# Filler products in the three waits between TensorE's first steps

## The reference

```python
x = x + mixer(ctx_1024, layernorm(x), ...)
x = x + ffn(layernorm(x), ...)

# mixer: 4 batches, 256 steps, 256 channels, 16 states a channel
x = einsum("bld,ed->bel", hidden, in_proj_w)          # 128 -> 256 channels
x = silu(causal_conv(x, conv_w, 4 taps) + conv_b)     # u
dt_low, B, C = split(einsum("bdl,ed->bel", x, x_proj_w))
dt = softplus(dt_proj_w @ dt_low + dt_proj_b)
state = state * exp(dt * A) + (dt * u) * B            # scan over the 256 steps
y = (sum over states of state * C + D * u) * silu(z)
# ffn: hidden 1024, activations rounded to 8 bits, weights to -1, 0, 1
h = layer_norm(gelu(silu(bitlinear(x, w1, b1))))
out = bitlinear(h, w2, b2)
```

## Time and profile before

| | us |
|---|---|
| median of 3 runs | 188.28 (187.84 to 191.62) |
| the profiled execution, its own time | 188.09 |
| its span, first to last instruction | 186.2 |
| PE, DVE, ACT, POOL busy in the span | 153.8, 155.1, 159.9, 128.8 |
| mean granted TensorE clock | 0.958 |

### The profile page before, as it was taken

One profiled execution on the slowest core, in us unless ns is written; L12 is line 12 of the kernel. 1 busy time (PEld: TensorE's weight loads), 2 busy tenths in 40 slices (PEclk: granted clock), 3 DMA queues, 4 the chain that ended last, 5 costly groups with the idle time before them and its releaser, 6 DMA issues.

```text
span 186.2 us, 3315 instructions
## 1 busy us (share of the span) xinstructions
PE 153.8 (83%) x1161; PEld 113.3 (61%) x1167; DVE 155.1 (83%) x225; ACT 159.9 (86%) x255; POOL 128.8 (69%) x117
## 2 busy tenths in 40 slices
PE   7868999999989989999778999975998946806762
PEld 4646978778777758667555778644856533305541
DVE  0769607898999999899999998999989399999951
ACT  2288968999999999999999999999999976997331
POOL 4002453799684059997999999789979968776860
PEclk9995799999999999999999999999999999995798
DMA  4919997228752400426260232300000000000011
GB/s 153 346 40 339 391 414 325 7 15 296 298 86 38 188 4 0 182 98 179 2 217 16 105 126 107 116 30 0 0 4 0 0 28 28 4 0 0 30 56 58
DMA packets 20192, 20.12 MB, mean 108 GB/s; under 512 B 13448, under 2 KB 16976, under 8 KB 19536
## 3 DMA queue, kind: packets, MB, share of 16 engines
q1 hardware_dynamic: 19584, 19.15, 31.2%
q10 hardware_dynamic: 592, 0.77, 1.2%
HBM read 17.70 MB, written 2.21 MB: 107 GB/s over the span
## 4 chain that ended last, share of the span: by engine, by line
PE 31%; ACT 29%; DVE 18%; issue 13%; POOL 6%; DMA 2%; DVEq 0%; ACTq 0%; POOLq 0%
ACT dA L681 12%; PE ps L517 8%; PE ps L454 7%; PE ps L555 6%; ACT L778 6%; DVE st L956 3%; DVE stats L1026 3%; POOL st L829 3%; PE ps L483 2%; DVE w_raw L1036 2%; DVE am L1051 2%; DVE w_raw L1040 2%; ACT w_raw L714 2%; ACT w_raw L718 2%; PE ps L465 2%
## 5 line engine op out<-in xcount | busy, mean ns | idle before, releaser
L829 POOL TENSOR_TENSOR st<-st,bc 128x1024 f32<-128x1024 f32 x32 | 76.3, 2400 | 21.3 <-DVE st L956 21.1
L956 DVE TENSOR_TENSOR_SCAN st<-dA,ps 128x1024 f32<-128x1024 f32 x32 | 72.2, 2277 | 10.9 <-PE ps L517 9.1
L681 ACT ACTIVATE dA<-dt,negA 128x255 f32<-128x255 f32 x128 | 52.9, 496 | 0.6 <-POOL negA L810 0.6
L517 PE MATMUL ps<-diagB,dtuT 64*128 64x128 f32 x512 | 44.0, 298 | 3.8 <-DVE st L956 2.7
L517 PEld LDWEIGHTS ps<-diagB,dtuT 64*128 64x128 f32 x512 | 33.6, 191 | 17.9 <-issue 8.7
L778 ACT ACT_TABLE_LOAD x29 | 37.2, 1283 | 0.5
L555 PE MATMUL ps<-id_f,st 128*128 128x128 f32 x256 | 33.9, 277 | 2.6 <-POOL st L829 2.6
L555 PEld LDWEIGHTS ps<-id_f,st 128*128 128x128 f32 x256 | 28.1, 141 | 5.7 <-POOL st L829 3.6
L616 PE MATMUL ps<-id_f,w_raw 128*128 128x128 f32 x64 | 10.4, 314 | 9.2 <-POOL w_raw L891 7.6
L592 PE MATMUL ps<-rows_sb,diag 128*128 128x512 f32 x32 | 15.3, 601 | 0.7 <-ACT w_raw L714 0.4
L616 PEld LDWEIGHTS ps<-id_f,w_raw 128*128 128x128 f32 x64 | 8.3, 161 | 11.2 <-issue 9.4
(11 more groups left out here) (107 smaller groups left out, 226.4 us busy)
## 6 DMA issues: line engine op xcount, KB each, us to landing
bc<-spread SPq DMA_DIRECT2D x16, 512.0 KB, 4.0
diagB<-dblocks SPq DMA_DIRECT2D x3, 1024.0 KB, 4.7
rows_sb<-rows SPq DMA_DIRECT2D x1, 1664.0 KB, 15.6
x_nat<-x SPq DMA_DIRECT2D x2, 512.0 KB, 7.2
w_raw<-w1T SPq DMA_DIRECT2D x1, 1024.0 KB, 9.0
w_raw<-w2T SPq DMA_DIRECT2D x1, 1024.0 KB, 11.6
dblocks<-diagB SPq DMA_DIRECT2D x1, 1024.0 KB, 14.5
out<-res SPq DMA_DIRECT2D x8, 128.0 KB, 1.7
```

Source lines behind the costliest of these rows:

```text
L517: mm = nc.tensor.matmul(o[:, i:i + SG // 2, t, r, :], dtuT[rows, b % 2, h, t, :], diagB[rows, b % 2, t, n, :], start=True, stop=True)
L681: e = nc.scalar.activation(dA[:, k % DA_RING, i * L + 1:(i + 1) * L], dt[:, h, b, 1:L], ACT.Exp, scale=negA[:, h, n:n + 1])
L829: tt(s, s, bc[:, ng].rearrange("p s l -> p (s l)"), ALU.mult).then_inc(prod_done, 1)
L956: nc.vector.tensor_tensor_scan(st[:, k % ST_RING, :], dA[:, k % DA_RING, :], slot(k), 0.0, ALU.mult, ALU.add).then_inc(scanned, 1)
```

## The change

`warm(22)` ahead of `xdbl(0)` becomes `warm(27)`, and two more calls are put in: `warm(5)` between `xdbl(0)` and `dtraw(0)`, and `warm(11)` between `b_cols()` and the first step of `PE_AT[0]`. That makes 21 more products. They wait for nothing but their turn on PE, and no other engine's program differs.

```diff
-WARM_FIRST, WARM_SECOND = 11, 22
+WARM_FIRST, WARM_SECOND, WARM_THIRD, WARM_FOURTH = 11, 27, 5, 11
...
             warm(WARM_SECOND)
             xdbl(0)
+            warm(WARM_THIRD)
             dtraw(0)
             b_cols()
+            warm(WARM_FOURTH)
             for k in range(UNITS + 1):
```

## The result

The changed kernel took 194.24 us (192.94 to 195.69, four runs) against 189.05 of the kernel before in the same comparison: a ratio of 1.030, 95% interval 1.018 to 1.041. I had forecast 187.4 with a range to 188.7. It is slower by 5 us where I saw 0.7 less. Four more runs of the same kernel, made later (after_again), gave 187.81, 190.68, 193.63 and 193.81, so the eight executions have their median at 193.7 and spread over 8 us.

What follows compares the result with a forecast made beforehand. PE was taken as the bound after 14.59, slowed by a clock dip. Of 2.5 us gained there, 0.67 was to survive the read into diagB at no filler cost: 188.09 - 0.67 + 0 = 187.42, say 187.4 us, range 185.5 to 188.7.

Steps and rivals of the forecast that it cites:

- The three waits and their fillers: PE's waits of 0.76, 0.66 and 1.28 us before the clock dip: filling costs 0, PE gains 2.5 us.
- Where it stops: At scale_b:8 the read into diagB lands at about 45.6; about 1.8 of 2.5 us becomes a DMA wait.
- the 0.67: Gain in us left at scale_b:8, 46.27 - 45.60, expected to reach the kernel's end.
- A price to weigh: Earlier bc loads beside the read into diagB might delay its landing; taken as none, 0.5 us as upper bound.
- Rival 3: PE's new wait from 43.8 to 45.6 brings its own clock dip: slower, 189 to 190.5 us; chance 0.08.
- Rival 1: The whole 2.5 us comes through past scale_b:8, 185.6 us; chance 0.15, including a part of it.
- Rival 2: No gain, 188.1 to 188.5 us: landing 0.7 us later, or the clock falls as before; chance 0.20 with another rival.
- The range: Whole kernel: 185.5 to 188.7 us, leaving out the slower case with a new clock dip and little else.

Runs made afterwards that it cites:

- hold_bc: The changed kernel with SyncE holding the four bc loads of batch 1 until the read into diagB has landed; 191.67 us.
- order_only: The changed kernel with GpSimd's product of unit 19 held until VectorE's two diagonal tiles are made, new wait unfilled; 190.75 us.
- wait_in_before: The kernel before, without the 21 products, with TensorE at scale_b:8 also waiting for the second bc load of batch 1; 199.3 us.
- zeros_first: The changed kernel with the zeros for dblocks written ahead of the weight loads and rows_sb loaded behind the read of batch 1; 186.48 us.
- after: The changed kernel itself in its first four runs, one of them profiled, against the kernel before; 194.24 us, ratio 1.030.
- first_two_waits: The changed kernel without the 11 products ahead of turn_half(0), so with warm(27) and warm(5) only; 189.47 us.
- fill_new_wait: The changed kernel with 24 more unread products between sum_states(4) and scale_b:8, in the new wait for the read; 190.98 us.
- last_wait_only: The kernel before with only the 11 products ahead of turn_half(0), none added in the other two waits; 189.29 us.
- fill_and_order: fill_new_wait with GpSimd's product of unit 19 also held until VectorE's two diagonal tiles are made; 189.94 us, ratio 1.002.

## Why the prediction was wrong, point by point

- **The three waits and their fillers: right.** The costs were taken at nothing and are 0.02 us; the gain was 2.5 us and is 2.7 (`xdbl:1` at 23.73, foreseen near 23.9). In the four profiles in which the first full clock came at 8.35 to 9.71, in place of 6.8, the filler cost 0.2 to 0.8 at `xdbl(0)`; I had put 0.1 to 0.3.
- **"Where it stops": right in kind, wrong in size.** PE came to `scale_b:8` at 43.7 (43.8 foreseen), and the wait has its place and cause. But I took the landing as fixed at 45.56, and it was 46.64. With that the 0.67 that I carried to the end is below nothing, -0.46. A landing read from one trace can't carry such a sum: in the ten profiles with this order of DMAs the read landed between 44.7 and 48.0.
- **"A price to weigh": the first step that failed.** I took 0 for the earlier `bc` loads beside the read, 0.5 at most; they cost 0.7 (the read took 5.4). That loads beside the read can cost it this much is shown by hold_bc and by the grouping of thirteen reads; how much it is varies (order_only, 0.2). What misled me was one read beside which a single load had run: it says nothing of two. The Trainium skill, "DMA: Bandwidth & Descriptors", section "Issuing engines are not separate DMA queues", had it right, that DMAs on the same 16 engines interleave, and the traces now agree (5.4 against 4.7). The other 0.4 stays unexplained: the four writes went out 0.4 earlier, but took 7.7 in place of 7.0 us to land. It is less than the read's issue moves by itself, 40.9 in the kernel before and 42.1 in wait_in_before, which are the same program up to there.
- **Rival 3 was the case, and I gave it 0.08.** Its mechanism was described as it came: the idle of PE, the clock that falls behind it, and a price of 1.5 to 3, measured as 3.17. The failed step is my ground against it, that dense work ahead of the wait protects the clock. In the changed kernel PE was busy 3.53 of the last 3.60 us ahead of the wait, and the clock fell 1.1 us after the wait had ended; after_again had a wait of 2.79 and no fall. The wait makes the fall possible, not certain. Of the four profiles of the 21 products with an unfilled wait for the read it came in one (3.05 us, and not behind 2.79, 2.58 and 1.48), and it came in wait_in_before (4.43). A wait of 1.8 us, as I foresaw it, can do it too: at unit 20, behind the held tile, PE waited 1.80 or 1.81 us in six profiles, and in three of them the clock fell. That is a large part of the chance, not 0.08.
- **A term that I didn't have:** the held tile, 2.1 us, and the low clock behind it, which made unit 23 another 2.0 later. My sum took for granted that behind 46 the engines keep their places to each other. By unit 19 the product had moved 0.2 us against the tile. The tile was held in all six profiles in which `scale_b:8` had to wait for a DMA and GpSimd's product wasn't held back, wait_in_before without the 21 products among them, and in none of the five in which it didn't have to wait. So it goes with the wait, not with the filler; how the wait moves the two against each other wasn't traced.
- **Rival 1, the whole 2.5 us,** is what zeros_first shows once the read is out of the way. **Rival 2** had the landing right: it said that 0.7 us later would be enough to take the gain, and it was 1.1 later. It had no price for what came behind.
- **The range** left out rival 3 by intent, and its upper end was sized by a rival that had none of the costs above.

## What to carry to other kernels

An engine that is made faster on the chain meets the next thing that doesn't depend on it; look up the landing of every DMA behind the gain, and take a margin under a microsecond as no margin. A new wait of TensorE of 2 to 3 us isn't worth its length alone: with the clock that may fall behind it, it cost 3 more here, more than the whole gain, and it shifted the engines so that VectorE was held as well. So first move the DMA (zeros_first), then add the filler; together they gave 1.3% (1.5% with the filler in the tail), where each alone gave nothing or a loss.

## What the runs showed of the hardware that I had not expected

- The clock falls after waits of the same length in one execution and not in another: behind the wait of 1.80 or 1.81 us at unit 20 it fell in after, first_two_waits and hold_bc, for 3.4 us each time, and not in after_again, fill_new_wait and wait_in_before. The length of the low clock varies too: 3.4, 6.8 and 10.2 us. The times spread over 8 us in the changed kernel and over 0.9 and 3.4 with the wait filled, but over 7 in the kernel before in one comparison. Part of the spread isn't the new wait's: a low clock of 6.8 us that starts between 149 and 163, in the tail, stands in four of the thirteen profiles (last_wait_only, fill_and_order, zeros_first, wait_in_before) and costs 1.8 to 2.2 us.
- A VectorE `tensor_scalar` of 128 columns that starts 0.13 us behind a GpSimd product took 2.38 us in place of 0.28, until the product had ended. It is an order of starts, not a load: 0.2 us decide over 2.1. The Trainium skill, "SBUF — State Buffer", section "Who interferes with whom", says that VectorE in a mode that takes both port pairs, which `tensor_scalar` can enter, contends with GpSimd, and that whoever issues first gets the shared pair for the whole instruction while the other is blocked. The rows of the changed kernel and of fill_and_order agree with it (2.38 with the product first, 0.28 with the tiles first); which mode the tile ran in no row shows.
- Filler at a low clock is no help but a delay: in last_wait_only 11 products took 2.51 us and made `turn_half(0)` 1.4 late.
